# First attention: the second squares of the weights are issued three half steps later on VectorE

## The reference, cut to what matters

```
q, k = layernorm(rope(x @ w_q)), layernorm(rope(x @ w_k));  v = x @ w_v
a = tril(einsum('bhnd,bhmd->bhnm', q, k) ** 4)
out = einsum('bhnm,bhmd->bhnd', a / sum(a, -1), v) @ w_out
x = layernorm(x + out)
```

## Time and profile before

| | us |
|---|---|
| median of 3 runs | 1612.76 |
| fastest and slowest of them | 1604.51, 1618.64 |
| span of the profiled execution, first to last instruction | 1538.8 |
| median less this span | 74.0 |
| busy in the span: TensorE, VectorE, ScalarE, POOL | 1310.7, 1041.4, 880.1, 681.3 |

### The profile page before, as it was taken

How to read it: one execution, slowest core, us unless ns; L and a number is a source line. 1 busy time by engine, 2 the same in 40 slices (tenths; PEclk the granted TensorE clock), 3 DMA queues, 4 the chain that set the end, 5 groups by cost and what they waited for, 6 DMA issues and landing times.

```text
span 1538.8 us, 26502 instructions
## 1 busy us (share of the span) xinstructions
PE 1310.7 (85%) x9451; PEld 834.2 (54%) x9451; DVE 1041.4 (68%) x2748; ACT 880.1 (57%) x1245; POOL 681.3 (44%) x862
## 2 busy tenths in 40 slices
PE   5577766776789999689999999999999988999995
PEld 4333453332567877444444554444444454899984
DVE  6767787768444355877887477777897456555685
ACT  2578726877433342337777576666667642566660
POOL 7477244657202103412333552442236637766661
PEclk9599986998989999759989999989999979999998
DMA  2591000012302100000000000000004445667876
GB/s 95 205 362 42 1 1 1 1 42 93 116 12 69 42 14 29 18 1 1 2 1 1 1 1 1 1 2 1 1 2 155 180 159 190 224 211 207 273 251 226
DMA packets 69143, 124.40 MB, mean 81 GB/s; under 512 B 7318, under 2 KB 55190, under 8 KB 67992
## 3 DMA queue, kind: packets, MB, share of 16 engines
q1 hardware_dynamic: 56728, 85.99, 17.2%
q0 software_dynamic: 12288, 36.72, 6.4%
HBM read 60.29 MB, written 62.39 MB: 80 GB/s over the span
## 4 chain that ended last, share of the span: by engine, by line
PE 53%; DVE 25%; ACT 10%; POOL 4%; issue 4%; DMA 3%; SPq 0%; POOLq 0%; DVEq 0%; ACTq 0%
PE psum L2465 10%; PE psum L2351 8%; PE psum L2440 6%; PE psum L2671 6%; DVE psum L3063 6%; PE psum L2570 4%; DVE probs L3083 4%; PE psum L2694 3%; ACT probs L2796 3%; PE psum L2412 3%; PE psum L2591 3%; PE psum L362 2%; PE psum L2454 2%; DVE neg_max L3066 2%; PE psum L2372 2%
## 5 line engine op out<-in xcount | busy, mean ns | idle before, releaser
L2794 ACT ACTIVATE probs<-psum,exp_shift 128x1024 f32<-128x1024 f32 (+1 forms) x320 | 325.8, 1032 | 143.3 <-PE psum L2440 139.0
L3063 DVE CUSTOM_DVE_ANT_0 psum<-psum,stage 128x512 f32<-128x512 f32 (+3 forms) x512 | 288.6, 618 | 88.4 <-PE psum L2412 88.3
L3720 POOL TENSOR_SCALAR_AFFINE_SELECT probs<-probs 128x512 f32<-128x512 f32 x192 | 140.8, 745 | 368.3 <-ACT probs L2794 266.3
L2440 PE MATMUL psum<-qt,kt 32*128 32x512 f32 (+5 forms) x1152 | 240.5, 452 | 48.6 <-ACT probs L2796 19.3
L2412 PE MATMUL psum<-kt,qt 32*128 32x512 f32 (+3 forms) x768 | 208.3, 457 | 20.2 <-DVE neg_max L3063 14.3
L3083 DVE TENSOR_TENSOR probs<-probs 128x1024 f32<-128x1024 f32 (+1 forms) x136 | 169.6, 1291 | 62.8 <-ACT probs L2796 62.5
L2440 PEld LDWEIGHTS psum<-qt,kt 32*128 32x128 f32 (+1 forms) x1152 | 106.7, 198 | 191.1 <-issue 75.6
L2465 PE MATMUL psum<-probs,v 128*32 128x256 f32 (+3 forms) x2048 | 177.1, 444 | 1.9 <-POOL probs L3720 1.9
L3791 POOL DMA_INDIRECT results<-sp_y,sp_row x128 | 126.1, 985 | 57.7 <-ACT sp_y L2855 29.0
L2796 ACT ACTIVATE probs<-psum 128x1024 f32<-128x1024 f32 (+1 forms) x160 | 140.5, 946 | 7.2 <-PE psum L2440 7.2
L3066 DVE TENSOR_REDUCE neg_max<-psum 128x1 f32<-128x256 f32 (+3 forms) x256 | 111.1, 483 | 26.3 <-PE psum L2412 26.0
(11 more groups left out here) (362 smaller groups left out, 2604.0 us busy)
## 6 DMA issues: line engine op xcount, KB each, us to landing
many_x<-blank SPq DMA_DIRECT2D x2, 10240.0 KB, 50.6
sp_xs<-many_x SPq DMA_DIRECT2D x64, 320.0 KB, 3.5
sp_w<-in_sparse SPq DMA_DIRECT2D x8, 1280.0 KB, 11.0
x_turned<-results SPq DMA_DIRECT2D x8, 768.0 KB, 5.9
sp_back<-results SPq DMA_DIRECT2D x8, 768.0 KB, 9.3
sorted_x<-blank SPq DMA_DIRECT2D x2, 1152.0 KB, 6.5
sorted_y<-y SPq DMA_DIRECT2D x18, 128.0 KB, 1.7
rows<-in_x SPq DMA_DIRECT2D x4, 512.0 KB, 6.8
```

The lines of the kernel that those rows point to most:

```text
L2440: inst = pe.matmul(psum[:, base - early:base + QCH - q0], A.kt[rows, k_slot, key * P:(key + 1) * P], A.qt[rows, q_slot, c * QCH + q0 - ear ...
L2794: inst = act.activation(dst, view, ACT.Exp, bias=exp_shift[:, 0:1])
L3063: inst = dve.tensor_tensor_reduce(src, src, causal_bf[:, (4 - cols) * P:4 * P], -1.0, -MASKED, ALU.add, ALU.min, dst)
L3720: pool.affine_select(out=dst, in_=dst, compare_op=ALU.is_ge, fill=0.0, base=0, pattern=[[0, 4], [1, P]], channel_multiplier=-1).then_inc(p ...
```

## The change

VectorE's second square leaves `scores` and becomes a unit of its own, `raise_weights`. Its event is still marked at the half step, but the unit is put into a list with the number of the half step (counted over a whole batch), and is issued after the scores of the half step that is three later (`SQUARED_LATER`). If a step is to be weighed while one of its squares is still in the list, the list is issued up to it first. All calls that the planner makes meanwhile, among them the normalization of the quad before, so stand ahead of up to three half steps' squares in VectorE's queue. The orders of the other engines stay as they are.

```diff
+SQUARED_LATER = 3
...
+                    to_raise, halves_scored = [], count()
+
+                    def raise_scored(before):
+                        while to_raise and to_raise[0][0] < before:
+                            _, unit = to_raise.pop(0)
+                            do("raise_weights", A=A, b=b, **unit)
+                            latest[raised.engine] = raised.event(L, b, *(unit[name] for name in ("quad", "c", "step", "h0")))
 
                     def weigh(entry):
                         quad, c, step, slot, ready, _ = entry
+                        while any(unit["p_slot"] == slot for _, unit in to_raise):
+                            raise_scored(to_raise[0][0] + 1)
...
                                 done = mark(raised, L, b, quad, c, step, h0)
+                            half_step = next(halves_scored)
...
                                 max_unit(unit[0], unit[1:])
+                            if poly and not on_act:
+                                to_raise.append((half_step, dict(quad=quad, c=c, step=step, h0=h0, p_slot=p_slot, slot=slot)))
+                            raise_scored(half_step + 1 - SQUARED_LATER)
                             if h0 == 0:
                                 yield
...
                     max_unit(A, before, maxima)
-                if A.softmax or on_act:
-                    return
+
+            def raise_weights(A, b, quad, c, step, h0, p_slot, slot):
                 view, dst = scored_view(A, c, step, h0, p_slot, slot)
                 q.wait_ge(exped, A.layer, b, quad, c, step, h0)
                 dve.tensor_tensor(dst, dst, dst, ALU.mult).then_inc(raised.by(A.layer, b, quad, c, step, h0), 1)
```

2 lines of the change are left out of this document (1 added, 1 removed).

## The result

The changed kernel takes **1634.85 us** (median of 4 runs, 1633.92 to 1636.85) against 1611.18 us (1604.51 to 1618.64) for the kernel before beside it: ratio **1.0145**, 95% interval 1.010 to 1.019. That is 23.7 us slower, where 6.6 us were forecast, and above the upper end of the range.

What follows compares the result with a forecast made beforehand. Prediction took ScalarE's wait for turn_q, behind VectorE's squares and normalization in the first attention, as the bound to relieve; its terms summed to +6.6 us on 1612.8, giving 1619.4 us, range 1605 to 1629.

Steps and rivals of the forecast that it cites:

- The aim: Batch 0: earlier normalization brings turn_q 1.3 us forward in quads 1 and 2 (-2.6 us), quad 3's scores earlier (-0.8 us).
- Hurried cut: Quad 0 of batch 0: second cut's subtractions stand ahead of the squares, delaying POOL's masks and cuts; +0.8 us.
- Layer norm in quad 0 of batch 1: Squares 5 to 7 fall behind the norm; POOL's mask and slow cuts follow late, delaying turn_q; +6.0 us.
- Quad 1 of batch 1: Norm passes squares 5 to 7, root 2.2 us earlier, about 1.4 us given back through the weighing; -0.8 us.
- Routing: Quads 2 and 3 of batch 1: routing work that waits delays squares and masks, less POOL's idle time; +1.3 us.
- End of batch 0: Squares 17 and 19 follow the add of project_out, so the last weighing ends later; +2.2 us.
- End of batch 1: Same loss behind the add, set against TensorE's 3.17 us wait for the half normalization; +0.5 us.
- POOL becomes the bound: Rival: turn_q waits for POOL, late masks push POOL's work at full price; +16.1 us, 1628.9 us; chance 0.13.
- first condition: Condition of the POOL rival: turn_q really waits for POOL, so the two turns in batch 0 gain nothing.
- place of decision: Where the POOL rival was to be decided: mask of quad 3's first step, POOL's 2.6 us idle time used up.
- The 74.0 us: Amount by which the median of the runs, 1612.76 us, lay above the profiled execution's span of 1538.8 us.

Runs made afterwards that it cites:

- experiment 13: Changed kernel, only normalization and layer norm passing pending squares, plus a VectorE wait for POOL's mask in quad 0 of batch 1; 1616.52 us, ratio 1.0037.
- experiment 2: Changed kernel, but only the normalization of the last quad passes the pending squares, all other work waits behind them; 1613.02 us, ratio 0.9999.
- experiment 4: Changed kernel, but pending squares are issued ahead of the layer norm in quads 0 and 1 of batch 1; 1627.97 us, ratio 1.0096.
- experiment 14: Changed kernel, but pending squares go ahead of routing in quads 2 and 3 of batch 1, some also ahead of that batch's end; 1631.50 us, ratio 1.0117.
- experiment 6: Changed kernel, but only the normalization and the batch ends (turned outputs' subtraction, project_out's add) pass pending squares, in batch 1 square 19 alone; 1621.31 us, ratio 1.0066.
- experiment 11: Changed kernel, only normalization, batch 0's half normalization and, in quad 0 of batch 1, layer norm (past squares 6 and 7 alone) pass squares; ratio 0.9999.
- experiment 12: Same as experiment 11, but in quad 1 of batch 1 the layer norm passes all pending squares, unlike intended; 1625.87 us, ratio 1.0022.

## Why the prediction was wrong

The kind of the effect was right, its size was not; the sum of +6.6 us should have been 24 to 27 us. By its own steps:

- **The aim, -2.6 and -0.8.** Right at each turn_q (138.61 to 137.20) and too large in sum: quads 1 to 3 of batch 0 together are 1.2 us shorter, not 3.4. What the prediction missed is that a quad that runs ahead loses about 0.7 us again where the next one begins (quads 1 and 2 each gain 1.2 at half step 8 and start the next quad with 0.5).
- **Hurried cut, +0.8.** 1.8 in the changed kernel, within that stage's scatter of 1.3.
- **Layer norm in quad 0 of batch 1, +6.0.** Right: 6.6. The way there differs a little. The prediction had a quick mask and slow cuts; the trace has a mask of 4.88 us and quick cuts, and experiment 13, which exchanges the two, moves it by 1.7 us.
- **Quad 1 of batch 1, -0.8: failed**, 4.0. The step "TensorE holds it ahead of the next scores: about 1.4 us is given back" priced the late square 5 through the weighing alone. Between square and weighing stands POOL's mask, which started behind the norm and took 4.94 us. In quad 0 I had followed this same path, here not. About half of the 4.0 are not the norm's: with the norm undone 1.9 stay, and the aim alone costs 2.3 here, 1.2 of it in a weighing at the lower clock (experiments 2 and 4).
- **Routing, +1.3: mis-sized**, 3.3 in quad 2 and 0.3 in quad 3. What it does to the end of batch 1 is not shown. The step took off POOL's idle time of 2.63 us in quad 3; but the wait falls into quad 2, where POOL idles 12.07 us for a square behind a subtraction that waits itself.
- **End of batch 0, +2.2: mis-sized**, 4.9. The term had the squares and half a weighing. It lacked the mask between them ("rounded"), which takes 1.47 us beside square 19 and leaves TensorE 3.54 us idle, and what followed from that: the granted clock fell to 0.50 and the weighing took 2.79 us instead of 1.50. 3.54 + 1.29 = 4.8. The second part is not certain: in experiment 14 the clock did not fall, and the same end lost 3.6.
- **End of batch 1, +0.5: failed, and the largest miss**, 7.1. The step counted TensorE's wait for the half normalization as a gain that offsets the loss. There was none: the wait for the half normalization went, but the last weighing still stood behind the add, the squares and the mask, as in batch 0. It started 3.1 us later against half step 19 and took 1.3 longer, and the granted clock stayed at 0.50 for the transposes and project_out behind it, 2.7 us more: 7.1 in all.

The misses are 2.2 + 1.0 + 0.6 + 4.8 + 2.3 + 2.7 + 6.6 = 20.2 us, which is 26.8 - 6.6. Two omissions make up most of it. What a late square costs was followed through POOL's queue in one of the places, and in the others only as far as the next instruction of TensorE. And no term had the granted clock, which fell behind TensorE's waits: 1.3 us at the end of batch 0 and 4.0 at that of batch 1. The rival "POOL becomes the bound" named the first mechanism; its chance was too low, and its price (+16.1 us) too, because it took the same short bounds for both ends and 0 for quad 1. Its first condition was wrong, as turn_q of quads 1 and 2 did not wait for POOL, and its place of decision too: the masks are late from quad 0 of batch 1 on.

The 74.0 us that the prediction put around the span were not there: they are the last stage of that one execution. They entered no term.

What stays open: the parts don't add. Alone beside the aim they cost 10.9 (layer norm), 14.0 (ends) and 9.6 to 13.4 us (routing), each taken from the whole 5.5, 6.7 and 8.3, and together 23.8. Three things are mixed in these numbers: a POOL that is already late may lose less by the next late square, the granted clock falls at other places and for other lengths, and the switch for the routing moves squares at the end of batch 1 too. How much is due to which was not taken apart. Not tested either is what the half normalization costs in batch 1.

## What to carry to other kernels

Moving work down an in-order queue moves every other item of that queue past it, so list them all and ask of each whether it waits for something: an item that waits makes the ready work behind it wait too. Follow the delayed result to its last consumer through each in-order queue on the way (here square, POOL's mask, POOL's cuts, TensorE), at every place and not only at the largest. A delay that lets TensorE idle can cost more than its length: in three of the four profiled executions with 3.54 us of idle time at the end of batch 0 the next products ran at or near half the clock.

## What the runs showed of the hardware

- A POOL mask of 128x512 elements that takes 0.64 us alone took 4.88 and 4.94 us beside an unbroken run of squares, and ended 0.5 us after the last of them (263.38 + 5.22 = 268.60, mask until 269.10). Elsewhere such masks, and cuts of 128x256, get through beside one square, in 1.1 to 1.9 us. What decides between the two was not found. One-input passes in float32 hold a mask in the same way (2.74 us).
- After the same 3.54 us without work at the end of batch 0, TensorE's granted clock went three ways. In the changed kernel and in experiment 4 it was 0.50 for the weighing and 1.00 behind it (4.9 us lost); in experiment 6 it was still at 0.50 until 200 us (7.9 us lost); in experiment 14 it stayed at 1.00 (3.6 us lost).
- Experiments 11 and 12 have one order of VectorE in quad 0 of batch 1 and agree within 0.01 us in ScalarE's half steps 0 to 15 there. Then TensorE idles 2.1 us in both; the granted clock stays at 1.00 in the one and is 0.55 to 0.59 in the other, from 270 to 278 us, and that quad ends 2.3 us later.
- One profiled execution of the kernel before went through its last stage in 1135.9 us, the 16 other profiled kernels here in 1199.7 to 1228.9, at 80 instead of 74 or 75 GB/s of transfers in the mean and a granted clock of 0.93 instead of 0.89 to 0.92.
